# Two-pass macaron transformer on one core: feed-forward sum, attention outputs and gated rounds in another order

## What is computed

```python
def attn_layer(x, Wqkv, qs, ksc, Wo):             # 16 heads of 64
    q, k, v = split(x @ Wqkv)
    q, k = rotary(l2norm(q) * qs), rotary(l2norm(k) * ksc)
    # windows of 32 queries see their own window and the one before, masked
    attn = softmax(8.0 * q @ k.T + mask)
    return (attn @ v) @ Wo

def ffn_layer(x, g, bln, W1, b1, W2, b2):          # inner size 341
    xn = (x - mean) / sqrt(var + 1e-5) * g + bln
    a, gate = split(xn @ W1 + b1)
    return a * gelu(gate) @ W2 + b2

def ffn(x):
    for i in range(6):
        x = attn_layer(shift_tokens(x), ...) + x   # half of the features come from the token before
        x = ffn_layer(shift_tokens(x), ...) + x
    return x

x = x + 0.5 * ffn(layernorm(x))
x = x + single_head_attention(layernorm(x))        # softmax over an axis of size 1: only v and w_o count
x = x + 0.5 * ffn(layernorm(x))
```

## Time and profile before

| | us |
|---|---|
| median of three executions | 3327.99 |
| fastest, slowest | 3326.37, 3331.45 |
| the profiled execution | 3330.9 |
| span of its instructions | 3329.1 |
| PE busy | 3079.3 (92%) |
| PE's weight loads busy | 2611.4 (78%) |
| DVE busy | 2689.4 (81%) |
| POOL busy | 2594.5 (78%) |
| ACT busy | 2361.0 (71%) |

### The profile page before, as it was taken

How to read it: one execution, slowest core, us unless ns; L and a number is a source line. 1 busy time by engine, 2 the same in 40 slices (tenths; PEclk the granted TensorE clock), 3 DMA queues, 4 the chain that set the end, 5 groups by cost and what they waited for, 6 DMA issues and landing times.

```text
span 3329.1 us, 150706 instructions
## 1 busy us (share of the span) xinstructions
PE 3079.3 (92%) x63810; PEld 2611.4 (78%) x63810; DVE 2689.4 (81%) x4403; ACT 2361.0 (71%) x4536; POOL 2594.5 (78%) x2894
## 2 busy tenths in 40 slices
PE   6999999999999999999779999999999999999997
PEld 4788888888878877877657888888788788788886
DVE  4888888888888878888558888888888888888884
ACT  4777777777777777777537777777777777777774
POOL 5987887888788878887349878878887888788773
PEclk8999999999999999999879999999999999999998
DMA  2222222221222222221102222222212212221211
GB/s 82 76 58 54 68 61 54 65 66 50 67 64 52 68 60 55 65 61 51 32 25 77 57 55 68 62 55 64 64 49 68 64 53 70 59 56 52 54 49 37
DMA packets 117860, 195.45 MB, mean 59 GB/s; under 512 B 23756, under 2 KB 36552, under 8 KB 117192
## 3 DMA queue, kind: packets, MB, share of 16 engines
q1 hardware_dynamic: 117192, 185.82, 20.9%
HBM read 33.71 MB, written 1.05 MB: 10 GB/s over the span
## 4 chain that ended last, share of the span: by engine, by line
PE 62%; POOL 13%; DVE 13%; ACT 6%; issue 6%; POOLq 0%; DMA 0%; DVEq 0%; ACTq 0%; SPq 0%
PE tr L985 8%; PE of_ps L970 7%; PE s_ps L933 5%; PE tr L946 5%; PE of_ps L1035 4%; POOL rotated L423 4%; PE qk_ps L871 4%; POOL rotated L452 3%; DVE ss_floor L724 3%; PE qk_ps L873 3%; PE qk_ps L872 3%; PE tr L898 3%; PE tr L871 3%; PE tr L911 2%; DVE fn_lo L772 2%
## 5 line engine op out<-in xcount | busy, mean ns | idle before, releaser
L423 POOL TENSOR_TENSOR rotated<-rotated 128x1024 f32<-128x1024 f32 x384 | 915.4, 2384 | 23.1 <-DVE rotated L717 23.1
L452 POOL TENSOR_TENSOR rotated<-rotated,rn 128x1024 f32<-128x1024 f32 x384 | 730.8, 1903 | 30.1
L429 POOL TENSOR_TENSOR prob<-prob,rden 128x512 f32<-128x512 f32 x384 | 437.8, 1140 | 391.5 <-DVE rden L749 391.5
L531 ACT ACTIVATE sq<-qk_ps 128x1024 f32<-128x1024 f32 x384 | 393.8, 1025 | 304.1 <-PE qk_ps L873 200.3
L711 DVE TENSOR_TENSOR rotated<-qk_ps,rot 128x1024 f32<-128x1024 f32 x384 | 469.0, 1221 | 140.4 <-ACT sq L531 125.9
L717 DVE TENSOR_TENSOR rotated<-qk_ps,rot 128x512 f32<-128x512 f32 x768 | 490.5, 680 | 0.0
L724 DVE TENSOR_REDUCE ss_floor<-sq 128x16 f32<-128x1024 f32 x384 | 464.0, 1208 | 0.4
L970 PE MATMUL of_ps<-pt,vs 64*64 64x32 f32 x12288 | 391.0, 222 | 68.2 <-DVE xa L788 65.1
L577 ACT ACTIVATE pt<-tr 128x512 f32<-128x512 f32 x384 | 230.0, 599 | 315.4 <-PE tr L946 315.2
L970 PEld LDWEIGHTS of_ps<-pt,vs 64*64 64x64 f32 x12288 | 325.7, 134 | 138.6 <-DVE xa L788 75.5
L985 PE MATMUL tr<-ot,wo 128*128 128x128 f32 x3072 | 408.9, 276 | 0.5 <-issue 0.5
(11 more groups left out here) (136 smaller groups left out, 7042.8 us busy)
## 6 DMA issues: line engine op xcount, KB each, us to landing
vs<-vn SPq DMA_DIRECT2D x384, 192.0 KB, 2.5
vs<-vtail SPq DMA_DIRECT2D x384, 64.0 KB, 2.0
vtail<-vn SPq DMA_DIRECT2D x384, 64.0 KB, 2.1
staging<-layer_wqkv_dram SPq DMA_DIRECT2D x72, 256.0 KB, 3.0
wo<-layer_wo_dram SPq DMA_DIRECT2D x12, 512.0 KB, 3.8
xs<-xa SPq DMA_DIRECT2D x48, 128.0 KB, 2.3
fs<-xa SPq DMA_DIRECT2D x48, 128.0 KB, 2.3
xs<-xa SPq DMA_DIRECT2D x48, 127.8 KB, 2.4
```

The source lines that it names most:

```text
L423: nc.gpsimd.tensor_tensor(rot_c[h], rot_c[h], rot_s[h], ALU.add).then_inc(rot_added, 1)
L429: nc.gpsimd.tensor_tensor(prob[h][:, :, :], prob[h][:, :, :], rden[h][:, :].unsqueeze(2).to_broadcast([P, 2 * PAIRS, KEYS]), ALU.mult).the ...
L452: nc.gpsimd.tensor_tensor(folded, folded, rn[:, :].unsqueeze(2).to_broadcast([P, 2 * UH, DH]), ALU.mult).then_inc(qkn_ready, 1)
```

## The change

1. The places of the gated rounds 1 and 2 (and 4 and 5) change: round 1 takes tr1, round 2 tr0. The waits of rounds 1 and 2 change with them, and `query_heads` of the next slot waits for the sixth hidden product.
2. In the slot behind the gated rounds, which is that of the down product, ACT runs `queries`, `keys`, `place_mask`, `outputs` and only then `exps`, `squares`, `first_guess`, `values`. In other slots the order stays.
3. DVE runs `add_ffn` in the slot of the down product (`DOWN_AT`) instead of at the start of the slot after (`ADD_AT`). It stands after `differences` and `square_sums` of unit n + 2, which is pulled ahead in this slot, and before `add_output`. PE's wait for it in `weigh_values` stays in the slot `ADD_AT`.

```diff
--- before.py
+++ after.py
@@ -161,8 +161,8 @@
         o_ps = of_ps[:, :, 0:HS]
         f_ps = of_ps[:, :, HS:SEQ]
         wide = [tr0[:, :], tr1[:, :], s_ps[:, 0, :], s_ps[:, 1, :]]
-        gated_up = [f_ps[:, 0, :], tr0[:, 0:HS], tr1[:, 0:HS]]
-        gated_gate = [f_ps[:, 1, :], tr0[:, HS:SEQ], tr1[:, HS:SEQ]]
+        gated_up = [f_ps[:, 0, :], tr1[:, 0:HS], tr0[:, 0:HS]]
+        gated_gate = [f_ps[:, 1, :], tr1[:, HS:SEQ], tr0[:, HS:SEQ]]
 
         consts_in = sem("consts_in")
         consts_ready = sem("consts_ready")
@@ -619,9 +619,13 @@
                     if live(p, n) and after_gated:
                         queries(n)
                         keys(n)
+                        if n > p * UPP:
+                            place_mask(n)
+                    if live(p, n - 2) and after_gated:
+                        outputs(n - 2)
                     if live(p, n - 1):
                         exps(n - 1)
-                    if live(p, n) and n > p * UPP:
+                    if live(p, n) and n > p * UPP and not after_gated:
                         place_mask(n)
                     if live(p, n + 2):
                         squares(n + 2)
@@ -630,7 +634,7 @@
                         keys(n)
                     if live(p, n + 1):
                         first_guess(n + 1)
-                    if live(p, n - 2):
+                    if live(p, n - 2) and not after_gated:
                         outputs(n - 2)
                     if live(p, n):
                         values(n)
@@ -803,18 +807,20 @@
                         spread(it)
                     if (it := ffn_of(p, n, NORM_AT + 1)) is not None:
                         normed_low(it)
-                    if (it := ffn_of(p, n, ADD_AT)) is not None:
-                        add_ffn(it)
                     if live(p, n + 2):
                         rotate(n + 2)
                     if live(p, n):
                         row_maxima(n)
                         differences(n)
+                    if (it := ffn_of(p, n, DOWN_AT)) is not None:
+                        if live(p, n + 2):
+                            square_sums(n + 2)
+                        add_ffn(it)
                     if live(p, n - 2):
                         add_output(n - 2)
                     if (it := ffn_of(p, n, GATED_AT)) is not None:
                         hidden(it)
-                    if live(p, n + 2):
+                    if live(p, n + 2) and ffn_of(p, n, DOWN_AT) is None:
                         square_sums(n + 2)
 
                 dve.wait_ge(xa_ready, ONE + SEQS * DEPTH * (p + 1))
@@ -893,7 +899,7 @@
                 else:
                     pe.wait_ge(vn_ready, ONE + U)
                 if (it := ffn_of(p, U - 1, GATED_AT)) is not None:
-                    pe.wait_ge(hid_ready, ONE + 2 * NCH * it + 5)
+                    pe.wait_ge(hid_ready, ONE + 2 * NCH * it + 6)
                 for a in range(PAIRS):
                     last = nc.tensor.transpose(tr0[:, a * P:(a + 1) * P],
                                                rot_c[h][:, 0, 2 * a:2 * a + 2, :].rearrange("p h d -> p (h d)"), ident[:, :])
@@ -1013,9 +1019,9 @@
                     c, m = CHUNKS[i // 2]
                     half = slice((i % 2) * HS, (i % 2 + 1) * HS)
                     if i == 1:
+                        pe.wait_ge(pt_ready, ONE + min(n, (p + 1) * UPP))
+                    if i == 2:
                         pe.wait_ge(y_added, ONE + min(n - 1, (p + 1) * UPP))
-                    if i == 2:
-                        pe.wait_ge(pt_ready, ONE + min(n, (p + 1) * UPP))
                     if i >= 3:
                         pe.wait_ge(hid_ready, ONE + 2 * NCH * it + i - 2)
                     for part in range(2):
```

## The result

The changed kernel took 3256.5 us in the median of four executions (3252.8 to 3258.2), the kernel before beside it 3328.9: a ratio of 0.978 with a 95% interval of 0.976 to 0.980, or 72.5 us less. The forecast was 3245.2 and the range 3222 to 3280. The profiled execution took 3255.1 us with a span of 3253.3, 75.8 less than the span before; the forecast's sum was 82.8.

The account below looks back on a forecast made before the run. TensorE was taken as the bound; 31 x 0.81, 13 x 0.10 and 44 x 1.31, less 1.2, gave 82.8 us off the profiled 3330.9, so 3248.1, or 3245.2 for the median; range 3222 to 3280.

Parts of the forecast that it names:

- What bounds the kernel: Whole loop: TensorE is the bound from the value products to the next gated rounds and keeps what it gains before them.
- Round banks: Gated rounds: round 3 starts right behind the first hidden product, gaining 0.81 us in 31 iterations and 0.10 in 13.
- the 31 iterations: Iterations of the 44 counted where TensorE waits for `add_output` in the gated rounds; claimed gain there 0.81 us each.
- the 13 late ones: Iterations of the 44 where TensorE comes late to the gated rounds and hardly waits for `add_output`; claimed gain 0.10 us each.
- ACT: Down product's slot: outputs 1.8 us earlier, exponentials 1.05 and squares 0.55 later; down product no longer waits for ACT.
- the new wait of 1.05: Slot after the down product: query transposes wait 1.05 us for `add_output`, in place of the value products' old 1.50.
- VectorE: Down product's slot: `square_sums`, sum and `add_output` follow `differences`; value products start 1.31 us earlier in 44 iterations.
- Slot A: Slot after the down product: VectorE just keeps up, GpSimd's gap before its scaling shrinks to 0.3 us; nothing costed.
- The rival that all of it is paid: VectorE's L696 is held by GpSimd in 22 iterations with a rotary table, all reaching TensorE: 12 us back, 3257; 10%.
- GpSimd as the bound: GpSimd's scaling in the down product's slot gains only 0.28 us and sets everything behind: 39 us gained, 3289; 14%.
- A shorter wait: Query transposes wait less, as exponentials don't hold up `rotate` or VectorE's steps overlap more: 24 us more, 3221; 7%.
- Slower: GpSimd's long operations hold VectorE's queue twice in the down product's slot, `add_output` ending 4.76 us later: 3453; 4%.

Follow-up runs that it names:

- the banks alone: Only the places of the gated rounds and the waits of rounds 1 and 2 and of `query_heads` changed, against the kernel before: ratio 0.995.
- the tables moved: The whole change with each rotary table one slot later, so that none lies ahead of L423 in the down product's slot: ratio 0.976, 3256.0 us.
- ACT's order and the tables later: Kernel before with only the new order of operations on ACT, and each rotary table one slot later: ratio 0.998.
- ACT's order alone: Kernel before with only the new order on ACT (mask and outputs ahead of exponentials) in the down product's slot: ratio 1.007.
- sum alone: Kernel before with only the feed-forward sum moved on VectorE into the down product's slot, old ACT order and old places of the rounds: ratio 0.977.

## Why the prediction came out as it did

- **What bounds the kernel.** Right. TensorE keeps what it gains before the value products: part two changed by 1 us in 2137 with the change. I had not seen that part two held 8 stretches at 1.2 GHz, which the change was to remove; the page's clock of 0.98 and a row at 1.00 hid them.
- **Round banks.** Right in mechanism: round 3 behind the first hidden product, in both kinds of iterations. The term was 0.81 and 0.10; measured 0.72 and nothing (22.2 us in the run with the banks alone, against 26.4). The difference is the start after a wait, in another round in each kind. In the 31 iterations it is round 2: it starts 0.06 after L761's end, as set, but its first matmul takes 0.39 instead of 0.28 and the next comes 0.23 later instead of 0.12 (626.10 and 626.33), so round 3 comes 0.17 after the first hidden product's end and not 0.06. In the 13 late ones it is round 3, which does start 0.06 after that end and then needs the same tenth more:

```profile
819.93 0.39 PE L1030 MATMUL of_ps<-fn_hi,w_hi 128*128 128x256 f32 x1
820.15 0.28 PE L1031 MATMUL of_ps<-fn_lo,w_hi 128*128 128x256 f32 x1
```

- **ACT.** The steps were right (outputs 1.8 earlier, exponentials and squares later), and the new wait of 1.05 stood there in full: measured 1.02 in the iteration shown, and 43.4 us in 45 places against 46 in 44. What I didn't do was to ask what the sum's move is worth without them. The order on ACT opens the wait of 1.0 to close one of 0.8, which makes part one 16.1 us longer, and the rest of its price, 10 us, comes in part two.
- **VectorE.** L792 and L761 came where they were put, all 0.1 later because of the rounds; from L761's end to the transposes it took 0.15 instead of 0.05. Together with the 0.09 of the rounds this makes 0.19 in each of 44 iterations: part one fell 74.3 us instead of 82.8. **These two sizes are what the sum had wrong**, both of them the time in which TensorE starts again after a wait.
- **Slot A.** Right. The gap of GpSimd was to be 0.3, it is 0.34; VectorE just keeps up, with 0.25 before L735. L700 is held in the iterations with a table, 1.07 against 0.64, and it costs nothing, as said. The rival that all of it is paid set 3257 and so meets the measured 3256.5 better than my 3245, but by chance: with the tables moved the hold is gone and the time stays (3256.0).
- **Rivals.** GpSimd as the bound: no, the transposes of its result still wait only where they did before (39.8 us in 68 places; in the trace before 39.0 in 67). A shorter wait: no. Slower: L728 took 1.21 and L792 0.74 under L423, so nothing was held there.
- **Not foreseen.** Six stretches at 1.2 GHz fewer (8 us won), and a scores group behind the value products that takes 7 us longer, with 16 to 19 more pauses in the whole span. They cancel, which is luck, so the span is off by 7 us, about what part one alone is off by (8), and the medians by 10.
- **Range.** The time lies in it, but the three rivals that lie outside (3289, 3221, 3453) add up to 25%, not to the two in ten that it was to leave out.

## What to carry to other kernels

Where several waits in a row are removed at once, price each removal alone and in pairs: the move of one operation behind the one that it was waiting for brought the whole gain by itself here, and a second move, made to shorten a wait that was worth 0.8 us, delayed the work on which a third wait then hung. A queue's order is judged by the last signal it gives, here `add_output`, not by the first wait it ends. And add a start-up tenth of a microsecond for every wait that stays on TensorE.

## What the runs showed of the chip

- **Short waits can halve TensorE's clock.** TensorE, otherwise 94% busy, idled 1.5 us before the value products in 42 iterations of the kernel before, and the clock fell to 1.2 GHz within 2.1 us of the restart in 7 of them (the eighth stretch lies at a pass's end, as do both of the change); with the banks alone it was 12 of 42. After 1.8 us, with ACT's order and the tables later, it was 23 of 39; after 2.5 us, with ACT's order alone, 19 of 20. With no wait there (sum alone) it was none, and none after the 1.0 us of the change. Each stretch cost 1.3 to 1.4 us in addition to the wait.
- **Held VectorE operations.** The subtraction with two SBUF inputs ended 0.55 us after GpSimd's L423 in every case in which it was held, and took up to 1.69 instead of 0.64 us. The sum (L792), with one of its tensors in PSUM, ran while GpSimd worked in 44 of 48 cases and always took 0.74 to 0.75 us.
- **A start after a wait costs TensorE a tenth of a microsecond.** The first matmul of a gated round takes 0.39 instead of 0.28 us when the round had to wait, and the next comes 0.22 to 0.23 instead of 0.12 later. The query transposes start 0.15 us after the end of the operation they waited for.
- **Pauses with no semaphore.** TensorE stops, mostly inside groups of 64 small matmuls (24 of 28 pauses in the change), for 0.1 to 0.9 us, at places of which many recur from execution to execution.
